# Another order of the MLP products around four variance spreads, and three token comparisons moved behind scatters on GpSimd

## The chip, the cores and the metric

The kernel runs on one core of a Trainium2 chip. The metric is the device time of one execution in microseconds (us); less is better. A core has five engines that run their own instruction streams and meet only at semaphores: TensorE (PE; its weight loads are PEld), VectorE (DVE), ScalarE (ACT), GpSimd (POOL) and SyncE (SP).

## The reference

`reference()` is one perceiver layer on `x` (4 x 128 tokens of width 128) with a context of 4 x 2048 rows: cross attention with 8 heads, then a 4 x 4 attention over the batch axis, then a mixture of 8 experts of which every token takes the best 2. Only the last part matters here, cut to its core:

```python
logits = x @ gate_W
probs = softmax(logits); rw, sel = top_k(probs, 2); rw = rw / rw.sum(-1)
h = gelu(einsum('th,ehf->etf', x, mlp_W1) + mlp_b1)            # experts 0..3
mlp_out = einsum('etf,efh->eth', h, mlp_W2) + mlp_b2
h0 = layernorm(x, g0, b0)                                      # experts 4..7
z = einsum('eti,eio->eto', rswaf(h0, grid), kan_sl_W0) + kan_sl_b0
h1 = layernorm(z, g1, b1)
kan_out = einsum('eti,eio->eto', rswaf(h1, grid), kan_sl_W1) + kan_sl_b1
out = einsum('eth,te->th', concat([mlp_out, kan_out]), w_full)
return x + out
```

`rswaf` is 1 - tanh(.)^2 at 8 grid points, so each of experts 4 to 7 (called KAN experts below) has two products over 8 basis functions with a layer norm between them. Experts 0 to 3 are MLPs with a GELU.

## The kernel before, in words

**Stages.** The program is written by hand, engine by engine, and each engine executes its stream in the written order; there is no scheduler. Cross attention fills the first 60 us, mixing over the batch and the gate the next few. From about 67 us the expert part runs, `ffn(r, again)`, written once per engine. Each expert has 160 slots for tokens (`SLOTS`); `gather(n)` on TensorE brings an expert's tokens into `xe`, `layer0(n)` is the first product of KAN expert n. The arguments n here count KAN experts 0 to 3 (experts 4 to 7 of the reference); for `to_rows`, `rows_out` and `keep_y`, n 0 to 3 are the MLP experts and 4 to 7 the KAN experts.

**Around the change, TensorE.** After the last `layer0`, TensorE issues `up(0)` and `up(1)` (L1174, first MLP products; each is 4 products, which the trace lists as 8 passes), `turn(6)` and `turn(7)` (L1122 and L1123, transposes that bring the tokens of the last two experts), then four `spread(n)` (L1165), each of which spreads the inverse standard deviation of KAN expert n over all partitions, mixed with `down(m)` (L1184, second MLP products), `up(2)`, `up(3)` and `to_rows(n)` (L1207, the transpose of an expert's result into token rows). Then come the four `layer1(n)` (L1195, second KAN products, 32 passes each), within each of which, after a quarter of it, stands one `to_rows`. At the end, `combine(e, half)` (L1262) and `combine_rest` (L1269) add the last two experts' rows into the output with the comparison tiles `own_slot` and `own_rest` as weights.

`spread(0)` waits for the inverse (`inverse_made`) and for all eight experts' tokens (`xe_kept`); `spread(2)` and `spread(3)` wait for `scaled`, since they reuse the two PSUM tiles. `up(m)` for m of 2 and 3 waits for the GELUs of expert m - 2 (`hid_kept`), `down(m)` for its own GELUs and, from m = 2, for `yT_kept`. `to_rows(0)` and `to_rows(1)` wait for all four `scaled`. 

**VectorE** (not edited) runs in this order: `keep_tokens(6)`, `keep_tokens(7)` (L1675), `scale(0)`, `scale(1)` (L1722, which reads the spread), `affine(0)` (L1729, two instructions), `scale(2)`, `scale(3)`, `affine(1)`, `keep_y(0)`, `keep_y(1)` (L1755, L1756), `rows_out(0)` (L1770), `affine(2)`, `keep_y(2)`, `rows_out(1)`, then the squares of the tanh tiles, `squares1` (L1745, 8 instructions per KAN expert, in pairs; `layer1(n)` waits for each pair), with `keep_y` (L1755 to L1764, in which L1755 and L1756 serve the MLP experts) and `rows_out` between them. `scale(n)` waits for `spread(n)`.

**ScalarE** (not edited): the 16 GELUs of `hidden(m)` (L785), then the tanhs of `basis1(n)` (L795), with `rows_out(4)` and later ones (L802) between them. `basis1(0)` waits for `affine(0)`; `basis1(1)` waits for the last MLP product, since its tiles lie on those of the GELUs.

**GpSimd and the end of the program.** GpSimd waits for the slots' numbers (`slots_in`), makes three comparisons of 128x512 (L589 twice and L590: which token does each slot of experts 6 and 7, and of the rest slots, hold), and then stores the rows of experts 0 to 5 and of two groups of rest slots in the table `y_table` in HBM by indirect DMA: `scatter_rows(0, n, y_stored)` for n = 0 to 5 (L596), `scatter_rest` after n = 3 and after n = 5 (L604). SyncE waits for all eight stores, reads `y_table` back (L528), VectorE adds the two halves and the residual (L1885, L1887), and then adds the TensorE sums half by half (L1892), each of which waits for `combined`. SyncE writes each half out (L531).

## Time and profile before

| what | value |
|---|---|
| median of 3 runs | 139.34 us (138.27 to 139.54) |
| profiled execution, its own time | 139.28 us |
| profiled execution, span of the core | 137.5 us |
| PE busy | 129.6 us (94%), 1047 matmul records |
| DVE busy | 106.7 us (78%) |
| ACT busy | 80.8 us (59%) |
| POOL busy | 40.0 us (29%) |
| mean granted TensorE clock | 0.992 of full speed |

The span goes from the first to the last instruction; 1.78 us of the execution's own time lie around it. All times in the views count from the span's start. A view that follows the order of time gives start, duration, engine, line and operation, then destination and source with their shapes, and how many alike were merged; in brackets stands how long the engine sat idle before, and who released it. The chain of work that ended last is found from the last instruction backwards.

### The profile page before, as it was taken

Reading aid. Unit: us, or ns where it says so; the run is one execution under the profiler, and the core shown is the slowest. Engines: PE = TensorE matmul, PEld = TensorE weight load, DVE = VectorE, ACT = ScalarE, POOL = GpSimd, SP = SyncE. Lnnn points to the kernel's source line nnn. Section 1 sums busy time; section 2 is a strip of 40 time slices with the busy share of each in tenths; the row PEclk is TensorE's granted clock in tenths of the full one; section 3 lists DMA queues with packets and bytes.
Section 4 is the critical chain, followed back from the end, with each engine's and each line's share of the span. In section 5 each row is a group of like instructions: output and inputs, shape, how many; then the busy total and the mean of one; then the engine's idle time right before and its main releaser. Section 6 shows DMA issues by size and latency. Waiting matters only on the chain.

```text
span 137.5 us, 2936 instructions
## 1 busy us (share of the span) xinstructions
PE 129.6 (94%) x1047; PEld 98.8 (72%) x1047; DVE 106.7 (78%) x346; ACT 80.8 (59%) x200; POOL 40.0 (29%) x54
## 2 busy tenths in 40 slices
PE   6999999999999999989999999999989999999980
PEld 2355565655655667669779999999769989999960
DVE  0479867999998999688989999951659699989132
ACT  0355967955865794514749997930373799921020
POOL 8387000000000000041600002785029386839100
PEclk9999999999999999999999999999999999999996
DMA  3999998993930001099900000111300010100142
GB/s 103 250 367 480 439 403 362 304 20 48 278 102 5 2 5 5 0 305 453 429 41 0 5 2 0 41 58 64 52 1 0 0 45 19 38 19 24 23 151 81
DMA packets 15237, 17.26 MB, mean 126 GB/s; under 512 B 8496, under 2 KB 13552, under 8 KB 14704
## 3 DMA queue, kind: packets, MB, share of 16 engines
q1 hardware_dynamic: 13984, 15.55, 36.7%
q0 software_dynamic: 512, 1.03, 2.3%
q10 hardware_dynamic: 720, 0.43, 1.3%
q8 instruction: 10, 0.16, 0.5%
q14 instruction: 11, 0.09, 0.2%
HBM read 14.53 MB, written 2.56 MB: 124 GB/s over the span
## 4 chain that ended last, share of the span: by engine, by line
PE 50%; DVE 22%; ACT 8%; DMA 7%; issue 4%; POOL 2%; POOLq 2%; SPq 1%; DVEq 0%
PE C L903 8%; DVE arena L1346 5%; PE D L890 5%; PE A L1139 5%; ACT arena L773 4%; PE A L1174 3%; PE D L1195 3%; DMA tokens_home<-x 3%; PE A L880 3%; DVE arena L1745 3%; PE C L1114 3%; PE D L1016 2%; PE D L1184 2%; ACT kw L748 2%; POOLq L68 2%
## 5 line engine op out<-in xcount | busy, mean ns | idle before, releaser
L682 ACT ACTIVATE arena<-C 128x512 f32<-128x512 f32 x32 | 18.9, 595 | 11.3 <-PE C L903 10.8
L1346 DVE CUSTOM_DVE_ANT_0 arena<-A,arena 128x512 f32<-128x512 f32 x32 | 20.2, 686 | 2.7 <-PE A L880 2.6
L903 PE MATMUL C<-cst,arena 128*128 128x128 f32 x128 | 20.5, 284 | 0.3 <-ACT arena L682 0.2
L903 PEld LDWEIGHTS C<-cst,arena 128*128 128x128 f32 x128 | 13.6, 141 | 9.0 <-issue 5.8
L1139 PE MATMUL A<-arena,kw 128*128 128x161 f32 x128 | 18.9, 302 | 0.0
L1195 PE MATMUL D<-arena 128*128 128x161 f32 x128 | 18.5, 301 | 0.3 <-DVE arena L1745 0.3
L1139 PEld LDWEIGHTS A<-arena,kw 128*128 128x128 f32 x128 | 17.7, 189 | 0.9 <-issue 0.5
L1195 PEld LDWEIGHTS D<-arena 128*128 128x128 f32 x128 | 17.8, 190 | 0.6 <-issue 0.5
L569 POOL TENSOR_TENSOR rstd<-var,mhalf 128x3 f32<-128x3 f32 (+1 forms) x2 | 1.4, 710 | 47.6 <-DVE var L1518 47.0
L585 POOL DMA_INDIRECT slot_table<-tokens_home,dest x8 | 8.2, 1026 | 19.3 <-DVE tokens_home L1640 17.1
L890 PE MATMUL D<-arena 128*32 128x128 f32 x256 | 13.4, 284 | 0.0
L1745 DVE TENSOR_TENSOR arena<-arena 128x320 f32<-128x320 f32 x32 | 13.4, 485 | 0.0
L596 POOL DMA_INDIRECT y_table<-arena,slot x6 | 11.4, 1902 | 6.6 <-DVE arena L1770 3.2
L795 ACT ACTIVATE arena<-arena 128x320 f32<-128x320 f32 x32 | 11.7, 470 | 0.0
L673 ACT ACTIVATE arena<-arena,nmxb 128x512 f32<-128x512 f32 x16 | 11.4, 718 | 0.0
L773 ACT ACTIVATE arena<-arena 128x160 f32<-128x160 f32 x32 | 7.7, 321 | 3.2 <-DVE arena L1672 3.2
L880 PE MATMUL A<-arena 32*128 32x512 f32 x64 | 9.1, 640 | 0.2 <-ACT arena L658 0.2
L890 PEld LDWEIGHTS D<-arena 128*32 128x32 f32 x256 | 5.1, 108 | 5.3 <-issue 2.8
L1114 PE MATMUL C<-arena,xf 128*128 128x160 f32 x48 | 8.1, 304 | 0.3 <-DVE arena L1664 0.3
L1114 PEld LDWEIGHTS C<-arena,xf 128*128 128x128 f32 x48 | 6.8, 189 | 0.7 <-DVE arena L1664 0.5
L1356 DVE TENSOR_SCALAR arena<-arena,nmxb 128x512 f32<-128x512 f32 x16 | 7.1, 484 | 0.3
L785 ACT ACTIVATE arena<-A,vec 128x160 f32<-128x160 f32 x16 | 4.9, 403 | 3.7 <-PE A L1174 3.7
(242 smaller groups left out, 226.4 us busy)
## 6 DMA issues: line engine op xcount, KB each, us to landing
kw<-KW SPq DMA_DIRECT2D x1, 4096.0 KB, 16.3
arena<-KW SPq DMA_DIRECT2D x1, 4096.0 KB, 13.6
mw<-MW SPq DMA_DIRECT2D x2, 1024.0 KB, 20.6
arena<-ctxT SPq DMA_DIRECT2D x4, 256.0 KB, 6.0
arena<-mask SPq DMA_DIRECT2D x1, 768.0 KB, 7.8
slot_table<-zeros SPq DMA_DIRECT2D x1, 640.0 KB, 7.2
y_table<-zeros SPq DMA_DIRECT2D x1, 512.0 KB, 6.8
arena<-y_table SPq DMA_DIRECT2D x2, 256.0 KB, 2.7
```

Of the source, the lines that this page charges most:

```text
L596: pool.indirect_dma_start(out=y_table, out_offset=bass.IndirectOffsetOnAxis(ap=slot[:, n, 0:1], axis=0), in_=yn[:, n], in_offset=None).the ...
L682: act.activation(PT[:, m % 4], C[m % 2][:, :], ACT.Exp).then_inc(probsT_kept, 1)
L773: i = act.activation(T0[:, n % 2, g], xe[:, n], ACT.Tanh, bias=tanh_bias(g))
L795: i = act.activation(T1[:, n % 2, g], zs[:, n], ACT.Tanh, bias=tanh_bias(g))
L880: last = mm(BANK[j], QM[32 * j:32 * j + 32, u, b], kT[32 * j:32 * j + 32, b], start=True, stop=True)
L890: last = mm(sums[VW * j:VW * (j + 1), g * P:(g + 1) * P], v[:, 4 * g + j], probsT[:, j * P:(j + 1) * P], start=False, stop=True, skip_grou ...
L903: last = nc.tensor.transpose(C[m % 2][:, j * P:(j + 1) * P], S[:, b % SBUFS, 4 * g + j, t * P:(t + 1) * P], ident)
L1114: last = mm(X[n % 2][:, 0:SLOTS], xf[:, i], onehot[:, n % 4, i], start=(k == 0), stop=(k == B - 1))
L1139: last = mm(Z[n % 2][:, c * (SLOTS + 1):(c + 1) * (SLOTS + 1)], kw0[:, n, g, c * P:(c + 1) * P], SQ0[:, n % 2, g], start=(g == 0), stop=(g ...
L1195: last = mm(Y[n % 2], kw1[:, n, c, g], SQ1[:, n % 2, g, c], start=(g == 0 and c == 0), stop=(g == G - 1 and c == 1))
L1346: last = v.tensor_tensor_reduce(S[:, b % SBUFS, h], BANK[j], mbias[:, b], 1.0, -NEG, ALU.add, ALU.max, mx0[:, b, h:h + 1])
L1745: ins = v.tensor_tensor(SQ1[:, n % 2, g:g + 2, c, 0:SLOTS], t, t, ALU.mult)
```

## The change

It makes two edits. On TensorE, in the first round (`again` false), the products and spreads behind `up(1)` and the two `turn`s stand in another order; the later rounds, which run only when an expert has more tokens than slots, keep theirs. On GpSimd the three comparisons become a function that is called after the scatter of expert 3 and of the first rest slots.

```diff
@@ GpSimd
             pool.wait_ge(slots_in, 80)
-            for e in range(SENT, EX):
-                nc.gpsimd.tensor_scalar(own_slot[:, e - SENT], token_row[:], token_of[:, e:e + 1], None, ALU.is_equal).then_inc(own_slot_made, 1)
-            nc.gpsimd.tensor_scalar(own_rest, token_row[:], token_r[:, 1:2], None, ALU.is_equal).then_inc(own_slot_made, 1)
+
+            def own_slots():
+                for e in range(SENT, EX):
+                    nc.gpsimd.tensor_scalar(own_slot[:, e - SENT], token_row[:], token_of[:, e:e + 1], None, ALU.is_equal).then_inc(own_slot_made, 1)
+                nc.gpsimd.tensor_scalar(own_rest, token_row[:], token_r[:, 1:2], None, ALU.is_equal).then_inc(own_slot_made, 1)
...
                 scatter_rows(0, n, y_stored)
                 if n == 3:
                     scatter_rest(0, 0, P, y_stored)
+                    own_slots()
                 if n == 5:
                     scatter_rest(0, 1, HALF, y_stored)
@@ TensorE
                 up(1)
-                if not again:
+                if again:
+                    spread(0)
+                    spread(1)
+                    down(0)
+                    spread(2)
+                    spread(3)
+                    up(2)
+                    down(1)
+                    up(3)
+                else:
                     turn(6)
                     turn(7)
-                spread(0)
-                spread(1)
-                down(0)
-                spread(2)
-                spread(3)
-                up(2)
-                down(1)
-                up(3)
+                    down(0)
+                    up(2)
+                    spread(0)
+                    spread(1)
+                    up(3)
+                    spread(2)
+                    spread(3)
+                    down(1)
                 to_rows(0)
```

TensorE's stream from `turn(7)` to the first `to_rows`, before. L1122 and L1123 are `turn`, L1165 is `spread`, L1184 is `down`, L1174 is `up`, L1207 is `to_rows`.

```order
L1122 MATMUL C<-cst,prod 128x128
L1123 MATMUL C<-cst,prod 128x32
L1165 MATMUL C<-arena,spread_w 128x160 x2
L1184 MATMUL D<-arena,mw 128x160 x4
L1165 MATMUL C<-arena,spread_w 128x160 x2
L1174 MATMUL A<-arena,mw 128x160 x4
L1184 MATMUL D<-arena,mw 128x160 x4
L1174 MATMUL A<-arena,mw 128x160 x4
L1207 MATMUL C<-cst,arena 128x128
```

The same stretch of TensorE's stream, changed (the line numbers are three higher: L1125, L1126, L1168, L1187, L1177, L1210):

```order
L1125 MATMUL C<-cst,prod 128x128
L1126 MATMUL C<-cst,prod 128x32
L1187 MATMUL D<-arena,mw 128x160 x4
L1177 MATMUL A<-arena,mw 128x160 x4
L1168 MATMUL C<-arena,spread_w 128x160 x2
L1177 MATMUL A<-arena,mw 128x160 x4
L1168 MATMUL C<-arena,spread_w 128x160 x2
L1187 MATMUL D<-arena,mw 128x160 x4
L1210 MATMUL C<-cst,arena 128x128
```

The first two spreads moved back behind `down(0)` and `up(2)`, the last two behind `up(3)`, and `down(1)` is now the last product ahead of the first `to_rows`. No product was added or taken away.

GpSimd's stream behind the eight stores into `slot_table`, before. L589 and L590 are the comparisons, L596 the scatters of experts' rows, L604 those of rest slots.

```order
L585 DMA slot_table<-tokens_home,dest 5120x132 x8
L589 TENSOR_SCALAR arena<-token_row,slot 128x512 x2
L590 TENSOR_SCALAR arena<-token_row,slot_r 128x512
L596 DMA y_table<-arena,slot 2304x128 x4
L604 DMA y_table<-arena,slot_r 2304x128
L596 DMA y_table<-arena,slot 2304x128 x2
L604 DMA y_table<-arena,slot_r 2304x128
```

The same, changed (the comparisons are now L591 and L592, the scatters L598 and L606):

```order
L585 DMA slot_table<-tokens_home,dest 5120x132 x8
L598 DMA y_table<-arena,slot 2304x128 x4
L606 DMA y_table<-arena,slot_r 2304x128
L591 TENSOR_SCALAR arena<-token_row,slot 128x512 x2
L592 TENSOR_SCALAR arena<-token_row,slot_r 128x512
L598 DMA y_table<-arena,slot 2304x128 x2
L606 DMA y_table<-arena,slot_r 2304x128
```

The three comparisons now stand between the fifth and the sixth of the eight scatters. VectorE's, ScalarE's and SyncE's streams are the same as before.

## Rows read from the trace of the kernel before

**Rows 1.** Page, part 4: the chain that ended last, by engine
```profile
PE 50%; DVE 22%; ACT 8%; DMA 7%; issue 4%; POOL 2%; POOLq 2%; SPq 1%; DVEq 0%
```

**Rows 2.** The chain that ended last, from 122 us on: start, us, what
```profile
122.06 0.38 ACT arena L802
...
122.70 0.51 POOL y_table L596
...
126.60 2.33 DMA y_table<-arena,slot_r
...
129.87 2.83 DMA arena<-y_table
...
132.82 0.70 DVE arena L1885
```

**Rows 3.** PE in order of time, 100 to 134 us
```profile
100.78 0.24 PE L1123 MATMUL C<-cst,prod 32*128 32x32 f32 x1
101.53 0.78 PE L1165 MATMUL C<-arena,spread_w 4*128 4x160 f32 x4 [0.51 <-DVE arena L1675]
...
106.53 1.25 PE L1174 MATMUL A<-arena,mw 128*128 128x160 f32 x8
107.62 0.27 PE L1207 MATMUL C<-cst,arena 128*128 128x128 f32 x1
...
110.79 1.34 PE L1195 MATMUL D<-arena 128*128 128x161 f32 x8 [0.28 <-DVE arena L1745]
...
117.24 4.56 PE L1195 MATMUL D<-arena 128*128 128x161 f32 x32
...
133.27 0.71 PE L1269 MATMUL A<-arena 64*128 64x128 f32 x4
```

**Rows 4.** DVE in order of time, 102 to 135 us
```profile
102.88 1.01 DVE L1729 TENSOR_SCALAR arena<-arena,hvec 128x160 f32<-128x160 f32 x2
...
104.96 1.14 DVE L1729 TENSOR_SCALAR arena<-arena,hvec 128x160 f32<-128x160 f32 x2
...
108.20 0.63 DVE L1729 TENSOR_SCALAR arena<-arena,hvec 128x160 f32<-128x160 f32 x2
...
116.93 3.30 DVE L1745 TENSOR_TENSOR arena<-arena 128x320 f32<-128x320 f32 x8
...
121.36 4.11 DVE L1745 TENSOR_TENSOR arena<-arena 128x320 f32<-128x320 f32 x10
...
134.28 0.75 DVE L1892 TENSOR_TENSOR arena<-arena,A 128x256 f32<-128x256 f32 x2
```

**Rows 5.** POOL in order of time, 102 to 128 us
```profile
102.21 3.13 POOL L589 TENSOR_SCALAR arena<-token_row,slot 128x512 f32<-128x512 f32 x2 [6.92 <-DMA slot_r<-slot_table]
105.33 1.55 POOL L590 TENSOR_SCALAR arena<-token_row,slot_r 128x512 f32<-128x512 f32 x1
109.06 1.05 POOL L596 DMA_INDIRECT y_table<-arena,slot  x1 [2.17 <-DVE arena L1770]
110.41 1.07 POOL L596 DMA_INDIRECT y_table<-arena,slot  x1 [0.30 <-issue]
111.79 2.78 POOL L596 DMA_INDIRECT y_table<-arena,slot  x1 [0.30 <-issue]
115.62 1.62 POOL L596 DMA_INDIRECT y_table<-arena,slot  x1 [1.05 <-DVE arena L1770]
117.54 1.11 POOL L604 DMA_INDIRECT y_table<-arena,slot_r  x1 [0.30 <-issue]
118.95 1.30 POOL L596 DMA_INDIRECT y_table<-arena,slot  x1 [0.31 <-issue]
122.70 3.60 POOL L596 DMA_INDIRECT y_table<-arena,slot  x1 [2.44 <-ACT arena L802]
126.60 1.06 POOL L604 DMA_INDIRECT y_table<-arena,slot_r  x1 [0.30 <-issue]
```

**Rows 6.** ACT in order of time, the GELUs of experts 0 and 1
```profile
99.96 2.39 ACT L785 ACTIVATE arena<-A,vec 128x160 f32<-128x160 f32 x8
```

## The prediction

> **What bounds the kernel now.** I read first the shares of the chain that ended last [rows 1]: TensorE has half of it, VectorE a fifth, and DMA and GpSimd 11% together. The share says which engines matter but not where, so the second view is the end of the chain in order of time [rows 2]. From 122.06 us it no longer runs over TensorE: ScalarE scales the rows of expert 5, GpSimd scatters them, the last scatter (rest slots) starts at 126.60 and has landed 2.33 us later, SyncE reads the table back (2.83 us from 129.87), and VectorE starts its first add at 132.82. I call this the table's path. The other path to the same adds is TensorE's: its last sum ends at 133.27 + 0.71 = 133.98 [rows 3]. The second of the two last adds, the one that needs it, starts at about 134.28 + 0.75 / 2 = 134.65 [rows 4]. So the table's path has no slack, and TensorE's has about 0.6 us. The change touches both: the products' order moves TensorE's path, and with it everything behind; the comparisons move into the middle of the table's path. The third view is GpSimd's own order [rows 5], the fourth TensorE's and VectorE's around 102 to 122 us [rows 3, 4].
>
> **Edit 1, the order of products.** Before, TensorE is done with the turns at 100.78 + 0.24 = 101.02, then waits 0.51 us for the last tokens, spreads at 101.53, and is busy until `to_rows(0)` at 107.62 [rows 3]. A product group (`up` or `down`, 8 passes) takes 107.62 - 106.53 = 1.09 us from start to start [rows 3]. Between 101.53 and 107.62 lie four such groups (4.4 us) and four spreads; so the spreads with their latencies are 6.09 - 4.36 = 1.7 us.
>
> Changed, `down(0)` can start at once. Its last product needs the fourth GELU; the eight GELUs take 2.39 us from 99.96, so the fourth is there at about 101.2 [rows 6], before TensorE reaches it. The order then gives: `down(0)` 101.05 to 102.15, `up(2)` to 103.25, spreads 0 and 1 to 104.1, `up(3)` to 105.3, spreads 2 and 3 to 106.1, `down(1)` to 107.3, `to_rows(0)` at 107.45 if VectorE is ready. The wait of 0.51 is gone, for a gain of at most 0.5 us on TensorE alone.
>
> VectorE pays for it: its `scale(0)` began right behind the spread at 101.53, and now begins behind a spread at 103.3, so 1.8 us later. But it gets back what it waited for later, and one thing more. Before, the two instructions of an affine took 1.01 and 1.14 us while the comparisons ran on GpSimd (102.21 to 106.88), and 0.63 when GpSimd was idle [rows 4, 5]. With the comparisons gone from there, affines 0 and 1 lose 0.38 + 0.51 = 0.89 us. I step VectorE forward: scales 0 and 1 from 103.85 to 104.65, `affine(0)` to 105.3, scales 2 and 3 from 105.5 to 106.4, `affine(1)` to 107.0, `keep_y(0)` to 107.4, which frees `to_rows(0)` at 107.45 or 107.5, `keep_y(1)` to 107.95, `rows_out(0)` to 108.3, `affine(2)` to 108.9. Before, `affine(2)` ended at 108.20 + 0.63 = 108.83 [rows 4]. Behind it `keep_y(2)` waits for `down(2)`, which follows `to_rows(0)` directly in both orders. So everything up to the first `layer1` product goes with `to_rows(0)`: 107.62 before, 107.47 now. This edit is worth -0.15 us at `layer1`, which began at 110.79 and waited 0.28 us for VectorE's squares [rows 3]. Bounds: no better than -0.6 (the stall of 0.51, with VectorE keeping up everywhere), no worse than +0.4, which is the same walk with affines of 1.0 us. ScalarE reaches its tanhs some 2 us earlier for expert 4, but that is worth nothing: VectorE makes their squares in the same place in its stream, and was behind ScalarE already.
>
> **Edit 2, the comparisons.** They took 3.13 + 1.55 = 4.68 us while GpSimd had nothing else: it then sat idle for 2.17 us [rows 5]. So taking them away from there frees nothing on GpSimd; the gain is the 0.89 us on VectorE, already counted. In the new place they stand behind the scatter of the first rest slots (ends 117.54 + 1.11 = 118.65) and ahead of the scatter of expert 4 (began 118.95). Behind them queue three scatters: expert 4, expert 5, last rest slots; and for the landing of the last waits SyncE, and for it the end. Sum: start 118.95 - 0.15 = 118.80; comparisons 4.68, to 123.48; gap 0.30; scatter of expert 4 1.05, gap 0.30, scatter of expert 5 1.05, gap 0.30 [rows 5]; the last scatter then starts at 126.48. Before it started at 126.60. That is -0.1 us, and it comes out so near to even because the scatter of expert 5 took 3.60 us before, where a plain one takes 1.05.
>
> That is the open price. The eight scatters took 1.05, 1.07, 2.78, 1.62, 1.11, 1.30, 3.60 and 1.06 us [rows 5], so over 1.05 they have 0, 0, 1.7, 0.6, 0.1, 0.25, 2.55 and 0. Nothing in the rows tells why three are long. If the long ones strike at random, two scatters (experts 4 and 5) ahead of the last have a sum over plain of 0 to 0.35 in four cases of ten, 0.6 to 0.85 in two, and 1.7 or more in the rest; the middle is 0.6. The bounds are 0 and 2.55 + 1.7 = 4.3. For the comparisons themselves the row is beside light VectorE work; in the new place VectorE squares without pause (8 instructions in 3.30 us, 10 in 4.11 [rows 4]). If each comparison waits out one square, 0.41 us, that is 1.2 us at most, and 0 at least; I take 0.2, near the row that exists.
>
> Table's path: -0.1 + 0.6 + 0.2 = +0.7 us. TensorE's path: -0.15, plus what the squares lose to the comparisons, less 0.6 of slack. The nearest row for that loss is the affines': 0.89 us over four instructions beside 4.68 us of comparisons. VectorE's lead over TensorE in the squares is as large: TensorE takes 32 passes in 4.56 us, so a pair of grid points (8 passes) each 1.14 us. The fourth pair of expert 5 is needed at 117.24 + 2 x 1.14 = 119.5 and made at 116.93 + 4 x 0.41 = 118.6; the third pair of expert 6 is needed at about 121.85 + 1.14 = 123.0 (TensorE's next run starts when these 32 passes end) and made at 121.36 + 2 x 0.41 = 122.2 [rows 3, 4]. So 0.8 to 0.9 us of lead hides 0.89 us of loss, and TensorE's path stays under the table's.
>
> Against the profiled execution: span 137.5 + 0.7, and 1.78 around it, gives 139.28 + 0.7 = 140.0 us. The profiled execution stands 0.06 under the median of the three runs, so nothing is added. The spread of those runs is 138.27 to 139.54; 1%, 1.4 us, is about what a measurement of this kernel tells from no change.
>
> **A rule that speaks against it.** The rows show that VectorE's one-input affines are lengthened by comparisons (1.14 against 0.63) and show no two-input square beside one [rows 4, 5]. The Trainium skill, page "SBUF — State Buffer", section "Who interferes with whom", says that a VectorE instruction with two SBUF inputs contends with a GpSimd instruction that reads SBUF, and that the one that started second waits for the whole of the other. The affines agree in kind but not in full: they lost 0.2 to 0.4 us each and not a comparison's 1.56. By the rule the time is that of the first rival.
>
> **The rivals.**
> First, slower: squares and comparisons exclude each other. They then alternate, a comparison of 1.56 us and one square of 0.41, so the three take about 3 x 1.56 + 2 x 0.41 = 5.5 us, in which VectorE makes 2 or 3 squares and not 13: it loses 4.1 us or more. Its lead is 0.8, so TensorE stalls 3.3 in `layer1` of experts 5 and 6. Off that goes the slack of 0.6: +2.7, 142.0 us. It decides as soon as the squares lose more than 0.8 + 0.6 + 0.7 = 2.1 us. For it: the affines, and the squares reading SBUF twice. Against it: the affines lost only a quarter of this.
> Second, slower: the long scatter stays with the seventh place or strikes expert 4's. Then the last scatter starts 2.55 later than in the plain sum: -0.1 + 2.55 + 0.2 = +2.65, 141.9 us. For it: two of the last six were that long. Against it: with expert 4's rows ready long before, the scatter of expert 5 no longer starts at the same moment as before.
> Third, faster: no scatter is long, comparisons cost 4.68, and `layer1` starts 0.6 earlier. Then the table's path is at -0.1 - 0.45 = -0.55, 138.7 us; with TensorE's path at -0.6 it ends there. More than 1% would need 1.4 us, for which neither path has the material, unless the comparisons run faster in the new place.
> Fourth, the order does nothing on the device: the time of `layer1`'s start is the same to 0.1 us and only the table's path speaks, 139.2 to 140.2. It is within the forecast's own range.
>
> **How the numbers follow.** Forecast (with the fourth) 0.5, own range 139.2 to 140.8; first rival 0.17, second 0.20, third 0.13. The first two are slower by over 1%, and of them a few land below the bound; the third is faster, mostly by less than 1%. So slower by over 1% 0.35, faster by over 1% 0.09, within 1% 0.56. The range for 8 in 10 goes from 138.6, the third rival, to 142.2, just past the first.
>
> **What would show it.** In the profile after: no TensorE wait at the first spread, and that spread near 103.3; affines 0 and 1 at 0.63 each pair; first `layer1` product at 110.6; comparisons from 118.8 to 123.5 or a little later; the last scatter's start near 127.3; the chain still over `y_table`. Wrong it would be if `layer1` began before 110.2 or after 111.2, if squares beside comparisons come much further apart than 0.41 us and TensorE waits for them, or if no scatter after the comparisons is over 1.3 us and the end still moves.

## The result, and the profile after

The changed kernel took 140.81 us (median of 4 runs, 140.38 to 140.99) against 139.44 us for the kernel before: a ratio of 1.0112, with a 95% interval of 1.0063 to 1.0161. That is slower by 1.4 us. It lies in the range that the forecast gave 8 chances in 10 (138.6 to 142.2), 0.8 us above its point and just above its own narrower range (139.2 to 140.8). The profiled execution took 140.69 us, with a span of 138.9. Some executions of each of these kernels run one or more per cent slower at a lower granted clock, and the ratios leave them out.

The front of the program is the same in both kernels, but it does not take the same time in each execution: `up(0)` began at 97.86 us in the trace of before and at 98.00 in that of the changed kernel, and at 97.5 to 99.9 in the experiments. So from here on places are also given counted from the start of `up(0)`, with a plus sign. Up to TensorE's last sum they repeat from trace to trace to a few hundredths where nothing on the way was changed, while the medians of the kernel before alone run from 139.4 to 141.3 us.

The chain that ended last in the changed kernel (start, us, what); its counterpart is [rows 2]:

```profile
118.02 1.11 POOL y_table L606
...
119.18 3.27 POOL arena L591 x2
122.45 1.54 POOL arena L592
...
127.03 3.06 DMA y_table<-arena,slot_r
...
130.60 0.37 SPq L528
...
131.03 3.09 DMA arena<-y_table
...
134.24 0.70 DVE arena L1897
```

As forecast, the chain runs over GpSimd and `y_table`, and now over the comparisons too. The last scatter starts at 127.03 (forecast: about 127.3), 0.43 us later than before. But from its start to VectorE's first add pass 7.21 us, where it was 132.82 - 126.60 = 6.22 [rows 2]: the scatter takes 3.06 us to land and not 2.33, the reading back 3.09 and not 2.83. These are 0.99 of the 1.42 us by which the first add is late.

TensorE in order of time, to be read against [rows 3]:

```profile
101.09 1.35 PE L1187 MATMUL D<-arena,mw 128*128 128x160 f32 x8
...
103.46 0.81 PE L1168 MATMUL C<-arena,spread_w 4*128 4x160 f32 x4
...
108.03 0.33 PE L1210 MATMUL C<-cst,arena 128*128 128x128 f32 x1 [0.46 <-DVE arena L1768]
...
111.27 1.34 PE L1198 MATMUL D<-arena 128*128 128x161 f32 x8 [0.29 <-DVE arena L1757]
...
122.59 0.33 PE L1210 MATMUL C<-cst,arena 128*128 128x128 f32 x1 [0.31 <-DVE arena L1776]
...
127.77 0.33 PE L1210 MATMUL C<-cst,arena 128*128 128x128 f32 x1 [0.28 <-DVE arena L1776]
...
134.83 0.71 PE L1281 MATMUL A<-arena 64*128 64x128 f32 x4
```

The wait of 0.51 us at the first spread is gone; `down(0)` fills it. In its place TensorE waits 0.46 us at `to_rows(0)`, for VectorE's `keep_y(0)`. `to_rows(0)` is at +10.03 (before +9.76), `layer1` at +13.27 (before +12.93): the new order costs 0.34 us. TensorE's last sum ends at 135.54, 1.56 us later than before, so between `layer1` and there another 1.08 us went. They went at two `to_rows` (122.59 and 127.77), which wait for VectorE's `keep_y` (L1776). That instruction stands behind the squares in VectorE's stream. Before, VectorE had itself waited half a microsecond between the eight squares and that `keep_y`:

```profile
120.74 0.16 DVE L1759 TENSOR_TENSOR arena<-D,vec 128x1 f32<-128x1 f32 x1 [0.51 <-PE D L1195]
```

VectorE in order of time, to be read against [rows 4]:

```profile
104.83 0.63 DVE L1741 TENSOR_SCALAR arena<-arena,hvec 128x160 f32<-128x160 f32 x2
106.12 0.89 DVE L1734 TENSOR_TENSOR arena<-arena,C 128x320 f32<-128x320 f32 x2 [0.66 <-PE C L1168]
106.93 0.63 DVE L1741 TENSOR_SCALAR arena<-arena,hvec 128x160 f32<-128x160 f32 x2
...
117.41 4.50 DVE L1757 TENSOR_TENSOR arena<-arena 128x320 f32<-128x320 f32 x8
...
119.02 1.20 DVE L1757 TENSOR_TENSOR arena<-arena 128x320 f32<-128x320 f32 x1
...
120.94 0.97 DVE L1757 TENSOR_TENSOR arena<-arena 128x320 f32<-128x320 f32 x1
...
122.44 1.02 DVE L1757 TENSOR_TENSOR arena<-arena 128x320 f32<-128x320 f32 x1
122.44 4.65 DVE L1757 TENSOR_TENSOR arena<-arena 128x320 f32<-128x320 f32 x10
```

The affines take 0.63 us a pair, as forecast. The eight squares take 4.50 us (before 3.30) and the ten 4.65 (4.11): 1.74 us lost. The three rows of a single square, taken out of those stretches, show how: a square takes 0.48 us otherwise, these three 1.20, 0.97 and 1.02, and the differences add up to the whole loss.

GpSimd in order of time, to be read against [rows 5]:

```profile
112.25 2.79 POOL L598 DMA_INDIRECT y_table<-arena,slot  x1 [0.30 <-issue]
116.10 1.62 POOL L598 DMA_INDIRECT y_table<-arena,slot  x1 [1.06 <-DVE arena L1782]
118.02 1.11 POOL L606 DMA_INDIRECT y_table<-arena,slot_r  x1 [0.30 <-issue]
119.18 3.27 POOL L591 TENSOR_SCALAR arena<-token_row,slot 128x512 f32<-128x512 f32 x2
122.44 1.55 POOL L592 TENSOR_SCALAR arena<-token_row,slot_r 128x512 f32<-128x512 f32 x1
124.16 1.05 POOL L598 DMA_INDIRECT y_table<-arena,slot  x1 [0.17 <-issue]
125.51 1.22 POOL L598 DMA_INDIRECT y_table<-arena,slot  x1 [0.31 <-issue]
127.03 0.91 POOL L606 DMA_INDIRECT y_table<-arena,slot_r  x1 [0.30 <-issue]
```

The three comparisons start at 119.18, 120.75 and 122.44. The first falls into a running square (119.02), and that one is long; the third starts together with its long square. The second starts 0.19 us ahead of its long square (120.94), and the square that was running then (120.54) took its usual 0.48. So each of the three goes with exactly one long square. The third and the fourth scatter are long again, the same to a hundredth; the seventh, 3.60 us before, is now 1.22.

### The profile page after: what moved, and what is told of

It is laid out like the page before. It is cut to its first block, busy times and chain, and to the rows that moved or that the text cites. A ratio compares the mean times of both kernels' runs of the same rounds, so it can differ in the third digit from the quotient of the medians.

```text
span 138.9 us, 2936 instructions
## 1 busy us (share of the span) xinstructions
PE 130.4 (94%) x1047; PEld 98.5 (71%) x1047; DVE 107.3 (77%) x346; ACT 80.9 (58%) x200; POOL 37.3 (27%) x54
## 3 DMA queue, kind: packets, MB, share of 16 engines
q0 software_dynamic: 512, 1.03, 2.3%
## 4 chain that ended last, share of the span: by engine, by line
PE 45%; DVE 22%; ACT 8%; DMA 8%; POOL 7%; issue 4%; POOLq 2%; SPq 1%; DVEq 0%
PE C L906 8%; DVE arena L1358 5%; PE D L893 5%; PE A L1142 5%; ACT arena L776 4%; PE A L1177 3%; DMA tokens_home<-x 3%; PE A L883 3%; PE C L1117 3%; DVE arena L1757 3%; POOL arena L591 2%; PE D L1019 2%; DMA arena<-y_table 2%; DMA y_table<-arena,slot_r 2%; ACT kw L751 2%
## 5 line engine op out<-in xcount | busy, mean ns | idle before, releaser
L1757 DVE TENSOR_TENSOR arena<-arena 128x320 f32<-128x320 f32 x32 | 15.2, 540 | 0.0
L598 POOL DMA_INDIRECT y_table<-arena,slot x6 | 8.8, 1462 | 16.3 <-DVE arena L1782 15.2
L805 ACT ACTIVATE arena<-C,slot 128x128 f32<-128x128 f32 x4 | 1.5, 368 | 11.6 <-PE C L1210 9.7
```

The costliest lines, as they stand in the source:

```text
L1757: ins = v.tensor_tensor(SQ1[:, n % 2, g:g + 2, c, 0:SLOTS], t, t, ALU.mult)
```

## The experiments

The table gives the places from the traces, all counted from `up(0)`. "7th" is the duration of the seventh scatter (expert 5's rows), "issue to landing" that of the last scatter, "add" the start of VectorE's first add of the table, "end" the end of the span. The landing in e4 can't be read from its trace.

| kernel | `layer1` | squares 8, 10 | last sum ends | 7th | last scatter | issue to landing | add | end |
|---|---|---|---|---|---|---|---|---|
| before | +12.93 | 3.30, 4.11 | +36.12 | 3.60 | +28.74 | 2.33 | +34.96 | +39.6 |
| changed | +13.27 | 4.50, 4.65 | +37.54 | 1.22 | +29.03 | 3.06 | +36.24 | +40.9 |
| e1_order_only | +13.26 | 3.29, 4.10 | +36.44 | 3.60 | +29.06 | 2.32 | +35.23 | +40.2 |
| e2_compares_only | +12.94 | 4.50, 4.65 | +37.21 | 1.21 | +28.69 | 3.35 | +36.35 | +41.0 |
| e3_write_only | +13.26 | 3.29, 4.10 | +36.46 | 1.30 | +27.86 | 3.10 | +35.40 | +40.3 |
| e4_new_none | +13.27 | 3.29, 4.09 | +36.46 | 1.18 | +26.66 | | +33.62 | +40.3 |
| e5_old_none | +13.02 | 3.30, 4.10 | +36.21 | 1.18 | +26.42 | 2.5 | +32.91 | +40.3 |
| e6_nudge | +13.27 | 4.50, 4.66 | +37.54 | 1.22 | +29.43 | 2.78 | +36.66 | +41.3 |
| e7_nudge_more | +13.26 | 4.51, 4.65 | +37.55 | 1.22 | +30.18 | 2.40 | +36.63 | +43.3 |
| c5_stall_filled | +12.58 | 3.30, 4.10 | +35.77 | 3.60 | +28.39 | 2.32 | +34.74 | +39.9 |
| c6_filled_split | +12.58 | 3.30, 4.10 | +35.77 | 3.68 | +28.47 | 2.25 | +34.78 | +41.7 |
| c7_filled_dve | +12.58 | 3.30, 4.11 | +35.76 | 3.59 | +28.38 | 2.43 | +34.73 | +40.1 |
| c9_dve_and_pads | +12.58 | 3.29, 4.10 | +35.77 | 3.59 | +28.38 | 2.44 | +34.85 | +39.5 |

The runs of the kernel before beside them spread from 138.1 to 143.8 us on these chips. Where a ratio is given it stands with its interval; where its interval is too wide for the effect, the places in the trace decide, and those are of one execution each. Behind the last add they don't repeat: from the start of the last of the four adds to the end of the span it takes 2.9 us in before, the changed kernel, e2, e6 and c9, 3.1 to 4.0 in e1, e3, e4, e5, c5 and c7, and 4.8 to 5.1 in e7, c6 and c8. So a place up to the last add speaks for an edit, and the end of one trace does not.

**e1_order_only**: the products' new order alone. Against the changed kernel (the call of `own_slots()` is gone too):

```diff
             pool.wait_ge(slots_in, 80)
-            def own_slots(): ...   # as in the change, called behind the fourth scatter
+            for e in range(SENT, EX):
+                nc.gpsimd.tensor_scalar(own_slot[:, e - SENT], ...)
+            nc.gpsimd.tensor_scalar(own_rest, ...)
```

> The new order of products alone; the comparisons stay ahead of the scatters. My theory: the order costs about 0.3 us at the start of layer1 (111.1 instead of 110.8), and since the comparisons still run from 102.2 to 106.9 us beside the affines, of which the first now starts at 104.8, one or two of them are lengthened again: layer1 starts at 111.2 to 111.7. Squares stay at 0.41 us apart. Time 139.8 to 140.3, the profile's end on the scatters. Rival (the order is the whole cost of the change): 140.8. Rival (the order is worth something and only the comparisons cost): 138.9 to 139.3.

Measured: 140.92 us, ratio 1.0033 (0.9985 to 1.0081). `layer1` starts at +13.26, exactly where the whole change has it, though one affine pair is lengthened here (0.93 us). That pair cost nothing, since VectorE then waited 0.36 us for the second spreads and not 0.66 as in the changed kernel. Everything behind moves with it: last sum and last scatter by +0.32, first add by +0.27. So by the trace the order costs 0.3 us: it gains nothing, as the second rival had it, and it is not the whole cost, as the first had it. The ratio alone can't tell the three apart.

**e2_compares_only**: the comparisons moved, the products as before. Against the kernel before:

```diff
+            def own_slots(): ...   # the three comparisons
...
                     scatter_rest(0, 0, P, y_stored)
+                    own_slots()
```

> The old order of products with the comparisons moved behind the fourth expert's scatter. My theory: affines 0 and 1 take 0.63 us a pair, layer1 starts 0.6 to 0.9 us earlier than before (about 110.0); then the squares lose about 1.7 us beside the comparisons and TensorE gives back 1.1; the last scatter starts near 126.0. Time 139.2 to 139.8. Rival (the order is the whole cost): this one is faster than before, 138.5. Rival (the move of the comparisons is the whole cost of 1.4 us): 140.8.

Measured: a median of 144.84 us over 6 runs, of 140.89 to 147.48, so there is no ratio; the profiled execution took 141.70. The trace:

```profile
103.85 0.63 DVE L1732 TENSOR_SCALAR arena<-arena,hvec 128x160 f32<-128x160 f32 x2
...
105.94 0.63 DVE L1732 TENSOR_SCALAR arena<-arena,hvec 128x160 f32<-128x160 f32 x2
...
107.71 0.35 DVE L1758 TENSOR_SCALAR arena<-D,vec 128x128 f32<-128x128 f32 x1 [0.72 <-PE D L1187]
```

Both affines are back at 0.63 us, and yet `layer1` starts at +12.94, as before. What the affines gave back stands as a wait of 0.72 us of VectorE for TensorE's `down(1)`. The squares lost 1.74 us and TensorE's last sum 1.09, as expected. The first add is at +36.35, 1.39 us later than before, though the last scatter starts no later (+28.69): 1.02 us of it is the landing (3.35), and the rest lies in reading the table back and around it. So with the comparisons in their new place alone, and in this one trace, the add is as late as in the whole change. My 139.2 to 139.8 was too low because I still booked 0.6 to 0.9 us of gain at `layer1`, and nothing for the landing.

**e3_write_only**: the changed kernel with memsets for the comparisons; the sums of experts 6 and 7 are left out.

```diff
             def own_slots():
-                (the three comparisons)
+                for k in range(3):
+                    nc.gpsimd.memset(arena[:, <792 free columns>], 0.0)
+                    nc.gpsimd.memset(arena[:, <the 512 columns of comparison k>], 0.0).then_inc(own_slot_made, 1)
```

> The changed kernel with the three comparisons replaced by six GpSimd memsets in the same place (512 and 792 columns, three of each), so the last two experts' sums are left out. Theory that a VectorE instruction with two SBUF inputs is held up by a GpSimd instruction that reads SBUF: the eight squares take 3.3 us and the ten 4.1 again, although GpSimd is busy writing; layer1 of the last experts is 1.1 us earlier than in the changed kernel; the end 139.3 to 139.8. Rival (any GpSimd traffic holds up the squares, or they are slow for another reason in that place): squares still lose over 1 us, end at 140.2 or more.

```profile
118.29 3.29 DVE L1758 TENSOR_TENSOR arena<-arena 128x320 f32<-128x320 f32 x8
...
122.71 4.10 DVE L1758 TENSOR_TENSOR arena<-arena 128x320 f32<-128x320 f32 x10
```

Beside 3.6 us of GpSimd writes the squares lose nothing, and TensorE's last sum ends at +36.46 and not at +37.54. So it is not the writing that holds up squares, but what a comparison does besides; of that, the reading of SBUF is the likely part, though no run has a GpSimd instruction that only reads. Through the squares it costs TensorE 1.08 us. The Trainium skill, page "SBUF — State Buffer", section "Who interferes with whom", has the first half of this as a rule (a VectorE instruction with two SBUF inputs contends with a GpSimd instruction that reads SBUF, not with one that only writes); this pair of traces agrees. The page's second half, that the later one waits for the whole of the other, is not what these traces show: in the changed kernel the long squares ended 1.04, 1.16 and 1.02 us after the start of their comparison, the comparisons took 1.58, 1.70 and 1.55, and the squares that came next ran beside the rest of the first and the third comparison at 0.48 us. Time: 141.03, ratio 1.0035 (0.9994 to 1.0076), higher than the 139.3 to 139.8 expected, of which 1.1 us is the level of these runs (140.53 for the kernel before and not 139.44). The rest: the table's path was not faster by the 1.2 us by which its last scatter started earlier, since landing (3.10) and reading back (3.38) were slow here too. That opened the next question.

**e4_new_none** and **e5_old_none**: no comparisons, new and old order; the sums of experts 6 and 7 are left out. Against the kernel before (e4 has the new order of products besides):

```diff
-            (the three comparisons, in the old place)
+            for k in range(3):
+                nc.gpsimd.memset(arena[:, <the 512 columns of comparison k>], 0.0).then_inc(own_slot_made, 1)
```

> The new order with the comparisons left out (three memsets of 512 columns in the old place instead, ahead of all scatters), so the last two experts' sums are left out. Gives the order by itself with GpSimd free. My theory: layer1 starts at 111.1 to 111.3 as in the changed kernel, squares 0.41 us apart, TensorE's last sum 0.3 to 0.5 us later than before, end near 139.6 to 139.9 if the seventh scatter is long as before, 139.4 if not. Rival (order worth nothing either way): 139.3; rival (order is the whole cost): 140.7.

> The kernel before with the comparisons left out (three memsets of 512 columns in their place), so the last two experts' sums are left out. Counted from the start of up(0): my theory, after the runs so far, is that the comparisons beside the affines cost nothing, since TensorE and not VectorE sets to_rows(0): layer1 starts at +12.9 us as before, although affines 0 and 1 take 0.63 each. The rival is the prediction's credit: layer1 starts 0.3 us or more earlier. The seventh scatter: 1.2 us, as in the four kernels without comparisons ahead of the scatters (3.6 with them). Then TensorE's sums end last, and the end comes 0.3 to 0.6 us earlier than before.

Measured: e4 140.89, ratio 1.0028 (0.9985 to 1.0071); e5 139.96 over 4 runs, without a ratio. With the new order `layer1` is at +13.27, with the old one at +13.02 without any comparison on GpSimd, no earlier than the +12.93 of before. This is the second witness that the comparisons in their old place cost TensorE nothing. In both the table's first add starts 1.3 to 2.1 us earlier than before. The last add then waits for TensorE, and is only 0.26 (e4) and 0.49 us (e5) earlier than before. Nothing of that reaches the end of the span (+40.3 against +39.6): SyncE took 1.55 and 1.72 us to issue the second half of the output, and 0.47 in the kernel before. Why, no run here shows. e5 also has an affine pair of 0.96 us beside memsets (0.63 otherwise), where e3's squares beside memsets kept their 0.48: GpSimd's writes hold up an affine and not a square.

**e6_nudge** and **e7_nudge_more**: the changed kernel, with a memset ahead of the last scatter.

```diff
                 if n == 5:
+                    nc.gpsimd.memset(arena[:, <512 free columns; 1400 in e7>], 0.0)
                     scatter_rest(0, 1, HALF, y_stored)
```

The trace's DMA records show what is peculiar in the slow landings. The last scatter is 32 packets on 16 engines. In the kernel before they come from 128.23 to 128.52 us, and nothing else moves. In the changed kernel 31 come from 128.52 to 128.81, and the last one, 4 bytes, at 129.17, where an instruction fetch of 8 KB (128.74, 0.43 us) ends. In e2 the late one comes at 129.82 (fetch 129.52, 0.31 us), in e3 at 128.87 (fetch 128.45, 0.42 us). The DMA queues of the changed kernel from 128.4 to 129.25 us (packets, MB, share):

```profile
q0 software_dynamic: 32, 0.03, 17.3%
q14 instruction: 1, 0.01, 3.1%
```

> The changed kernel with one GpSimd memset of 512 columns (0.5 us) put ahead of the last scatter, on columns that nobody reads. Theory (collision): the last scatter lands late in the changed kernel because an instruction fetch of 8 KB occupies one of its DMA engines just then (0.43 us), so a scatter that starts 0.5 us later misses it: issue to landing 2.3 to 2.5 us instead of 3.1, and the landing comes at the same time as in the changed kernel or up to 0.3 earlier, not 0.5 later. Rival (three scatters close behind one another, or comparisons ahead of them, make the last land late): 3.1 us or more again, landing 0.5 us later.

> The changed kernel with a GpSimd memset of 1400 columns (about 1.2 us) ahead of the last scatter. In e6_nudge the memset put the last scatter's packets only partly behind the fetch (they came from 30.93 to 31.26 us after up(0), the fetch from 30.76 to 31.27), and it landed in 2.78 us, between 2.33 and 3.1. Theory (collision with the 8 KB fetch): now the packets come after 31.5, nothing shares their engine, and issue to landing is 2.3 to 2.5 us. Rival (close scatters or comparisons before make it late): 2.8 to 3.3 us.

The last scatter of e6, then of e7, in the chain of each:

```profile
126.97 2.78 DMA y_table<-arena,slot_r
```

```profile
129.55 2.40 DMA y_table<-arena,slot_r
```

e6: 140.74, ratio 1.0087 (1.0045 to 1.0129); the packets met the end of the fetch, and 0.28 us of the excess went. e7: one run, of 144.5, so only its trace counts; the packets were clear of every fetch, and the scatter landed in 2.40 us. It started 1.15 us later than in the changed kernel, and the reading back could be issued 0.49 us later. So the rival (close scatters) falls. In all the traces the landing took 2.8 to 3.35 us in the four in which a fetch met the packets, and 2.25 to 2.5 in the nine others whose landing can be read. The excess is larger than the wait of the one packet, 0.36 us. The rest lies behind it: from the end of the last packet to the semaphore it takes 0.4 us in the nine, and 0.86 to 1.03 in the four with a fetch. Why that part grows too, no run shows.

**c5_stall_filled**: the old order, with the stall filled by one product group only, and `up(2)` between the two pairs of spreads.

```diff
+                    down(0)
                     spread(0)
                     spread(1)
-                    down(0)
+                    up(2)
                     spread(2)
                     spread(3)
-                up(2)
                 down(1)
                 up(3)
```

> The kernel before, but down(0) ahead of the first two spreads and up(2) between the pairs of spreads, so that TensorE's wait of 0.51 us is filled and VectorE gets its spreads only 0.7 us later, not 1.9. Theory (TensorE sets to_rows(0), and the changed order lost by letting VectorE start too late): to_rows(0) and layer1 come 0.3 us earlier than before, counted from up(0): layer1 at +12.6 us. Time 0.3 us under before. Rival (any spread behind a product costs as much as the wait it fills): layer1 at +12.9 or later.

```profile
100.92 1.35 PE L1184 MATMUL D<-arena,mw 128*128 128x160 f32 x8
102.20 0.81 PE L1165 MATMUL C<-arena,spread_w 4*128 4x160 f32 x4
...
107.24 0.27 PE L1207 MATMUL C<-cst,arena 128*128 128x128 f32 x1
...
110.41 1.34 PE L1195 MATMUL D<-arena 128*128 128x161 f32 x8 [0.29 <-DVE arena L1753]
```

Measured: 139.02 against 139.57, ratio 0.9966 (0.9927 to 1.0004). `layer1` is at +12.58, as expected: 0.35 us earlier than before and 0.69 earlier than in the changed kernel. No wait stands at the spread or at `to_rows(0)`. At `layer1` the same idea of filling the stall gains 0.35 us with one product group and loses 0.34 with two. The last adds start 0.22 us earlier than before, since they still wait for the table (reading it back took 2.98 us here and 2.83 before). The ratio's interval just takes in no change.

**c6_filled_split**: c5, with one comparison in GpSimd's gap ahead of the seventh scatter. **c7_filled_dve**: c5, with all comparisons on VectorE behind its last squares. **c8_dve_only**: the same in the kernel before. **c9_dve_and_pads**: c7, with three memsets that nobody reads where the comparisons stood.

```diff
# c6
                 scatter_rows(0, n, y_stored)
+                if n == 4:
+                    (the third comparison)
# c7, c8, c9 (the comparisons on GpSimd are gone)
                 squares1(3, range(6, 8))
+                if not again:
+                    dve.wait_ge(token_rows_in, 64)
+                    for e in range(SENT, EX):
+                        v.tensor_scalar(own_slot[:, e - SENT], ...)
+                    v.tensor_scalar(own_rest, ...)
```

> As c5_stall_filled, and the third comparison moved into GpSimd's gap of 2.4 us between the sixth and the seventh scatter, two staying ahead. Theory: one comparison makes the squares lose 0.6 us, which VectorE's lead of 0.8 over TensorE covers; the last scatter is not delayed by it. Whether the seventh scatter stays at 3.6 us with two comparisons ahead I can't say: if it does, the time is that of c5_stall_filled; if it falls to 1.2, the end is TensorE's and 0.3 to 0.6 us earlier than before. Rival (the comparison in the gap costs as in the changed kernel): 0.3 us or more over c5_stall_filled.

> As c5_stall_filled, with the three comparisons made by VectorE behind its last squares, in its wait of 3 us for the last layer1, and none on GpSimd. Theory: they take 1.0 to 1.7 us there and hide; the squares keep 0.41 us; the seventh scatter takes 1.2 us as in every kernel without comparisons ahead of the scatters, so the table's first add can start 2 us earlier and waits for nothing; TensorE's last sum ends at +35.8 us from up(0), and the last add follows at once, 0.9 us earlier than before. Time 0.4 to 0.9 us under before, if writing the two output halves does not take longer than there (it did in the two kernels where the first half's add came early). Rival (the freed table's path buys nothing, because the end of the output moves with something else): as c5_stall_filled, 0.3 us under before.

> The kernel before with the comparisons on VectorE behind its last squares, none on GpSimd, the order of products as before. Theory: layer1 at +12.9 us from up(0), TensorE's last sum at +36.1, last add right behind it: 0.3 to 0.6 us under before. Rival: as before, since TensorE's sums were only 0.5 us behind in any case and the output's two halves now crowd.

> As c7_filled_dve, and three GpSimd memsets of 512 columns that nobody reads where the comparisons stood, as in the two kernels with a short seventh scatter. My theory that comparisons ahead of it make the seventh scatter long has fallen with c7_filled_dve (no comparison on GpSimd, 3.59 us all the same); what is left is that something ahead of the scatters in GpSimd's stream decides it. If memsets there do it: seventh scatter 1.2 us, the table's first add 2 us earlier, TensorE's last sum ends at +35.8 us from up(0) and the last add follows it. The end then comes 0.5 us before that of c5_stall_filled if the write of the output costs what it does there, or not earlier at all if it costs what it did in e4_new_none. If the seventh scatter stays at 3.6 us, the two kernels had it short for another reason, which stays open.

Measured: c6 ratio 1.0002 (0.9964 to 1.0039). Its one comparison fits the gap: no square is long, where I expected 0.6 us of loss, and up to the last add its places are those of c5. That is partly the moment: the comparison starts at 119.88, just as the last of the eight squares has ended (119.81), VectorE then waits 0.51 us for TensorE, and the next square, at 120.94, takes 0.48 us beside the comparison's last half microsecond. c7 ratio 0.9981 (0.9926 to 1.0037): the three comparisons take 1.3 us on VectorE, in its last wait, and `layer1` and the last sum are those of c5. But the seventh scatter takes 3.59 us with no comparison on GpSimd at all, so my theory of it fell, and with it the 2 us. c9 was to tell whether memsets there make it short: they don't, 3.59. Its ratio is 0.9910 (0.9857 to 0.9963), the only one of all that excludes no change on the fast side; but up to the last add its trace differs from c5's and c7's by 0.12 us or less, and from before's by 0.35 us at the last sum and 0.11 at the first add, so more than about 0.3 us of it can't be shown as its doing. c8 is inconclusive: 0.9983 (0.9904 to 1.0063), and its trace was disturbed, as the last section shows.

## Why the prediction was right, and where it was not

**The time and the side.** 140.0 was forecast, with 56% on within 1% and 35% on slower by over 1%; measured are 140.81 and +1.1%, at the edge between the two cases. It is in the wide range, but that is luck in good part: the sum got there with errors that cancel. All three signs that the prediction named for being wrong came true: `layer1` began after 111.2 (111.27, of which 0.14 is the later front), squares beside comparisons came further apart and TensorE waited behind them, and no scatter behind the comparisons is over 1.3 us (1.05, 1.22 and 0.91) and the end still moved. Of the rivals that change the time, the first had a mechanism right and its size wrong; the second (a long scatter behind the comparisons) and the third (faster) did not come, nor did the fourth (the order does nothing).

**Edit 1, the order.** Forecast -0.15 us at `layer1`, bounds -0.6 and +0.4; measured +0.34. The step that failed is "scales 2 and 3 from 105.5 to 106.4": the second pair of spreads was issued at +7.48 (105.48), where +7.44 was worked out, but VectorE could start on it 0.64 us later (106.12), and the sum had 0.2. Between the first spread (103.46) and its scale (104.03) lie 0.57 us. I had about that much, 0.55, for the first pair and left most of it out for the second. The 0.44 us make `keep_y(0)` late, and TensorE waits 0.46 for it.

**The credit of 0.89 us for the affines.** The size was right (0.63 a pair) and its worth was nil. (Singly, the affines of before took 0.36 and 0.74 us, then 0.48 and 0.74, so they were not each lengthened by 0.2 to 0.4 as the prediction says.) Before, `to_rows(0)` followed `up(3)` on TensorE without a wait [rows 3], so VectorE was not what it waited for; e2 shows `layer1` unmoved with both affine pairs freed, and e5 with one of them. The row to read was TensorE's at `to_rows(0)`, which has no bracket.

**The squares.** The first rival named the mechanism, with a chance of 0.17, and the forecast took a small loss (0.89, hidden by a lead of 0.8). The loss was 1.74 us, and TensorE's stall 1.08, so 0.66 was covered. The sum looked for the lead in the wrong place, though: it compared the pairs of squares with the `layer1` passes that need them, and TensorE stopped at `to_rows`, for the `keep_y` behind the squares. What covered the 0.66 there is VectorE's own wait of 0.51 us ahead of that `keep_y`, and some 0.2 us between its end and `to_rows`. The rival's size, 4.1 us by full exclusion, was too large by more than twice, since each comparison holds up one square and not all that would fall in its time. It did not set the end: TensorE's last sum ended at 135.54, and the second of the last adds, which needs it, came at 136.03.

**The queue on GpSimd.** Start of the last scatter: forecast about 127.3 (+29.4), measured 127.03 (+29.03). The terms "comparisons 4.68 + 0.2" came to 122.44 + 1.55 - 119.18 = 4.81. The term "0.6 for long scatters at random" failed: they are not random. The third took 2.8 us and the fourth 1.6 in every trace of the study. The seventh takes 3.6 or 1.2 to 1.3: 3.6 in before, e1 and c5 to c9, 1.2 to 1.3 in the changed kernel and e2 to e7. What decides it is open: without any comparison on GpSimd it is long in c7, and with three memsets ahead of the scatters it is long in c9 and short in e5, so neither is the condition. The change's one real gain is here: the seventh is short, which pays for half of the 4.8 us of comparisons, and the other half fits in the wait for expert 5's rows.

**What was not in the sum.** Landing +0.73 and reading back +0.26, nearly 1 us together, which is most of what the end moved by besides the order. The term that the sum put at nothing is thus the larger one, and the +0.7 that it had, for scatters and comparisons ahead of the last scatter, measured +0.29. e6 and e7 show the landing's part to be a meeting with an instruction fetch. In the traces that fetch goes roughly with TensorE's progress: counted from `up(0)` it came 1.48 us later than before in the changed kernel and 1.41 in e2, where TensorE's last sum was late by 1.42 and 1.09, and so it moved into the scatter's time. So the squares' loss may have cost the end something after all, by moving the fetch; but e3, which lacks that loss, met a fetch too. Since this takes a coincidence within 0.3 us, it could as well have gone the other way. The reading back's 0.26 us I have not isolated: over the traces it took between 2.80 (e1) and 3.38 us (e3, e6).

In sum, from `up(0)` to the first add (+1.28): the order 0.3; the comparisons' move -0.05 at the start of the last scatter (e2); +0.7 by the landing and +0.3 by the reading back, both as they fell in this one trace.

## What to carry to other kernels

Before crediting a shortened instruction, look at the consumer's row: if the consumer has no wait there, the credit is nil, however large the saving. When a stall is filled, work out how much later the next engine gets its input: with one product group the first spreads came 0.70 us later than before and `layer1` gained 0.35, with two they came 1.79 later and it lost 0.34. And here GpSimd's comparisons did no harm beside VectorE's waits and its short one-input instructions (c6), and did harm beside its squares, which have two SBUF inputs; moving them cost time there, and no gain from moving them can be seen in c6 or c7 either.

## What the runs showed of the hardware that was not expected

Beside VectorE's squares a GpSimd comparison of 1.55 to 1.70 us lengthened exactly one of them, by 0.5 to 0.7 us, and let the rest pass, in each of the four traces that have all three comparisons there. In c6, where no square ran in its first microsecond, it lengthened none. Where an instruction fetch of 8 KB met the packets of the 32-packet scatter, the landing took 0.4 to 1.0 us longer.

The same meeting shows at the end of the program, where the table above has its largest differences. In c6 all but one of the output's packets were through at +38.69, and the last, 4 bytes, came at +40.12, where an instruction fetch of 16 KB (+38.64 to +40.11) ended; the span ended 5.1 us after the last add's start and not 2.9. In e7 and c8 17 packets of the output came behind such a fetch, at +41.75 and +42.00. In the kernel before this fetch began at +38.83, just as the last packets went, and in the changed one at +40.21, 0.06 us behind them.

In c8's trace `layer1` started at +14.61 and not near +12.9. TensorE from `up(2)` on, and the busy times by stretch (us, then PE, PEld, DVE, ACT, POOL, each with its instructions, granted clock, DMA share, GB/s):

```profile
106.30 2.34 PE L1171 MATMUL A<-arena,mw 128*128 128x160 f32 x8
```

```profile
99.90:105.00 5.10, 4.59 (x30) 3.97 (x30) 2.98 (x7) 4.01 (x10) 0.00 (x0) 1.00 0.14 4
105.00:112.00 7.00, 7.00 (x39) 6.66 (x38) 3.26 (x13) 2.36 (x8) 0.00 (x0) 0.76 0.00 0
```

From 105 to 112 us the granted clock was 0.76 on average; in finer stretches it is 0.50, the lower of the two levels (1.2 GHz and not 2.4), from 106.5 to 109.9 us, and 1.00 or close to it on both sides. TensorE had been busy for 4.59 of the 5.10 us up to 105 and then without a break. Eight passes took 2.34 us where they take 1.25 otherwise, and the stretch made `layer1` 1.68 us late. Such a stretch and the output's last packets are two reasons for the wide spread of the runs, and for reading places in the trace and not medians alone.
